# A hybrid attention and expert block: the steps of a block put in another order on TensorE, VectorE and ScalarE

## What is computed

```python
x = x + window_attention(group_norm(x))      # windows of 8x8 tokens, 12 heads of 8, softmax
t = to_tokens(x)
t = t + linear_attention(layer_norm(t))      # feature map exp(t) or t+1 on k and v; k^T v per image and head
t = t + mixture_of_experts(layer_norm(t))    # 4 experts, top 2, gelu, hidden width 384
```

```python
attn = softmax(einsum('wntd,wnsd->wnts', q, k) * SCALE)
out = einsum('wnts,wnsd->wntd', attn, v) @ w_proj + b_proj
```

## Time and profile before

| | us |
|---|---|
| runs shown | 718.61, 720.95, 728.96 |
| median | 720.95 |
| the profiled execution, whole | 715.83 |
| its span, first to last instruction | 714.1 |
| PE / VectorE / ScalarE / GpSimd busy in it | 627.9 / 530.8 / 472.0 / 99.8 |
| granted TensorE clock, mean of the span | 0.962 |

### The profile page before, as it was taken

The page is one execution under the profiler, slowest core; times in us unless marked ns, Lnnn a source line. Parts: engine busy times, 40 slices in busy tenths (PEclk is TensorE's granted clock), DMA queues, the critical chain, the costliest instruction groups (busy, mean ns, idle before and its releaser), DMA issues.

```text
span 714.1 us, 19890 instructions
## 1 busy us (share of the span) xinstructions
PE 627.9 (88%) x6885; PEld 476.8 (67%) x6885; DVE 530.8 (74%) x1364; ACT 472.0 (66%) x843; POOL 99.8 (14%) x146
## 2 busy tenths in 40 slices
PE   1557789899999999999998779999999999999996
PEld 1235576677667776767776667677777777777774
DVE  6334577677777887778976676788878778888875
ACT  1235657557766777766776546877777777777773
POOL 5000122210222211222101311000000000001000
PEclk9999869979999999999999859999999999999999
DMA  2447644463555545456542003122222221222210
GB/s 43 93 100 154 117 85 89 75 114 82 100 97 91 109 101 101 95 84 116 100 90 34 1 5 89 45 56 62 58 58 58 55 55 55 55 55 55 62 48 22
DMA packets 53452, 52.99 MB, mean 74 GB/s; under 512 B 38761, under 2 KB 48811, under 8 KB 51884
## 3 DMA queue, kind: packets, MB, share of 16 engines
q1 hardware_dynamic: 53420, 52.57, 35.2%
HBM read 39.24 MB, written 12.71 MB: 73 GB/s over the span
## 4 chain that ended last, share of the span: by engine, by line
PE 64%; DVE 15%; DMA 8%; SPq 5%; issue 4%; POOL 2%; ACT 1%; DVEq 0%; ACTq 0%; POOLq 0%
PE ps L787 12%; PE ps L789 12%; PE ps L788 12%; SPq L393 5%; DMA k_split<-parts_dram 5%; DVE neg_max L1183 4%; PE ps L659 3%; PE ps L680 3%; PE ps L742 2%; PE ps L752 2%; PE ps L712 2%; DMA parts_dram<-parts_room 2%; PE ps L781 2%; PE ps L632 2%; PE ps L726 2%
## 5 line engine op out<-in xcount | busy, mean ns | idle before, releaser
L1469 DVE TENSOR_TENSOR hidden_part<-hidden,hidden_part 128x512 fp32r<-128x512 f32 x192 | 139.6, 746 | 53.3 <-ACT hidden_part L1104 41.0
L1103 ACT ACTIVATE hidden<-ps 128x512 f32<-128x512 f32 x192 | 115.1, 600 | 62.7 <-PE ps L789 62.7
L1104 ACT ACTIVATE hidden_part<-ps 128x512 fp32r<-128x512 f32 x192 | 113.9, 593 | 0.0
L987 ACT ACTIVATE probs<-ps 128x768 f32<-128x768 f32 x64 | 51.9, 811 | 52.0 <-PE ps L680 52.0
L787 PE MATMUL ps<-in_part,up_part 97*128 97x512 f32 x192 | 78.9, 411 | 0.0
L787 PE MATMUL ps<-hidden_part,down_part 128*96 128x512 f32 x192 | 76.7, 399 | 1.7 <-DVE hidden_part L1469 1.6
L788 PE MATMUL ps<-in_part,up_part 97*128 97x512 f32 x192 | 76.8, 400 | 0.0
L1183 DVE TENSOR_REDUCE neg_max<-ps 128x12 f32<-128x768 f32 x64 | 60.8, 950 | 21.1 <-PE ps L659 20.9
L789 PE MATMUL ps<-in_part,up_part 97*128 97x512 f32 x192 | 76.2, 397 | 0.0
L789 PE MATMUL ps<-hidden_part,down_part 128*96 128x512 f32 x192 | 75.9, 395 | 0.0
L788 PE MATMUL ps<-hidden_part,down_part 128*96 128x512 f32 x192 | 75.4, 393 | 0.0
(11 more groups left out here) (161 smaller groups left out, 1223.0 us busy)
## 6 DMA issues: line engine op xcount, KB each, us to landing
mix_rows<-mix_dram SPq DMA_DIRECT2D x16, 768.0 KB, 5.0
parts_dram<-parts_room SPq DMA_DIRECT2D x32, 288.0 KB, 2.8
q_packed<-parts_dram SPq DMA_DIRECT2D x96, 96.0 KB
k_split<-parts_dram SPq DMA_DIRECT2D x192, 48.0 KB
x_in<-in_x SPq DMA_DIRECT2D x64, 48.0 KB, 4.3
x_res<-in_x SPq DMA_DIRECT2D x64, 48.0 KB, 4.2
out<-out_sb SPq DMA_DIRECT2D x64, 48.0 KB, 1.9
t_all<-in_L_ffn_w SPq DMA_DIRECT2D x2, 576.0 KB
```

Of the source, the lines that this page charges most:

```text
L987: act.activation(probs[p % 2][:, :, :].rearrange("p (b h) t -> p b (h t)", b=2), pT_ps, ACT.Exp, scale=SCALE).then_inc(probs_ready, 1)
L1103: act.activation(hidden[n % 4][:, :], up_ps[n % 4], ACT.Gelu).then_inc(hidden_ready, 1)
L1104: act.activation(hidden_parts[n % 4][0][:, :], up_ps[n % 4], ACT.Gelu).then_inc(hidden_part1, 1)
L1469: dve.tensor_tensor(hidden_parts[n % 4][1][:, :], hidden[n % 4][:, :], hidden_parts[n % 4][0][:, :].bitcast(F32), ALU.subtract).then_inc(h ...
```

## The change

Only the order of the calls in the three `iteration` functions is changed. No instruction is added or taken away, and no semaphore, buffer or wait value changes.

- PE: `oT1` 0 before `max_transpose` 0; `attn_sum` and `shifted_scores` 0 before `scores_of` 2; `max_transpose` 1 before `scores_of` 3; `shifted_scores` 1 before `y1`; `max_transpose` 2 before `gvar`; `shifted_scores` 2 before `pv` 0; `max_transpose` 3 and `pv` 2 before `q_proj`; `shifted_scores` 3 before `h1_transpose`; `k_proj` before `gate`.
- ScalarE: `exp_kv` 1 before `copy_v` 0, `second_part` 1 behind `copy_v` 0; `exp_probs` 0 before `copy_xT`; `pack_max` 3 before `first_part` 0.
- VectorE: `third_part` 0 first, `third_part` 1 from behind `max_parts` 0 to behind `normalise` 0; `features` 0 before `max_parts` 0, `features` 1 before `maxima` 1; `mask_attn` before `maxima` 2; `max_parts` 3 from behind `norm2` to ahead of `residual1`.

```diff
--- before.py
+++ after.py
@@ -812,36 +812,36 @@
                 when(project, v_proj, *j, 0)
                 when(tail_a, pv, *a, 3)
                 when(attend, scores_of, k, u, 1)
+                when(tail_a, oT1, *a, 0)
                 when(attend, max_transpose, k, u, 0)
-                when(tail_a, oT1, *a, 0)
                 when(project, v_proj, *j, 1)
+                when(tail_b, attn_sum, *b)
+                when(attend, shifted_scores, k, u, 0)
                 when(attend, scores_of, k, u, 2)
-                when(tail_b, attn_sum, *b)
                 when(norm, x_transpose, *n)
                 when(tail_a, oT1, *a, 1)
-                when(attend, shifted_scores, k, u, 0)
                 when(tail_b, attn_times_proj, *b)
+                when(attend, max_transpose, k, u, 1)
                 when(attend, scores_of, k, u, 3)
-                when(attend, max_transpose, k, u, 1)
                 when(tail_b, fold, *b)
                 when(tail_a, oT2, *a)
                 when(norm, gmean, *n)
+                when(attend, shifted_scores, k, u, 1)
                 when(tail_b, y1, *b)
+                when(attend, max_transpose, k, u, 2)
                 when(norm, gvar, *n)
-                when(attend, shifted_scores, k, u, 1)
                 when(tail_a, y0, *a)
-                when(attend, max_transpose, k, u, 2)
+                when(attend, shifted_scores, k, u, 2)
                 when(attend, pv, k, u, 0)
-                when(attend, shifted_scores, k, u, 2)
                 when(attend, pv, k, u, 1)
+                when(attend, max_transpose, k, u, 3)
+                when(attend, pv, k, u, 2)
                 when(norm, q_proj, *n)
                 when(tail_b, h2_transpose, *b)
-                when(attend, max_transpose, k, u, 3)
-                when(attend, pv, k, u, 2)
+                when(attend, shifted_scores, k, u, 3)
                 when(tail_a, h1_transpose, *a)
+                when(norm, k_proj, *n)
                 when(tail_b, gate, *b)
-                when(norm, k_proj, *n)
-                when(attend, shifted_scores, k, u, 3)
                 when(tail_a, kv, *a, 0)
 
 
@@ -1047,19 +1047,19 @@
                         step(*args)
 
                 when(tail_a, exp_probs, *a, 3)
+                when(project, second_part, *j, 0)
                 when(tail_b, exp_kv, *b, 0)
-                when(project, second_part, *j, 0)
+                when(tail_b, exp_kv, *b, 1)
+                when(project, copy_v, *j, 0)
                 when(project, second_part, *j, 1)
-                when(project, copy_v, *j, 0)
-                when(tail_b, exp_kv, *b, 1)
                 when(attend, pack_max, k, u, 0)
                 when(project, copy_v, *j, 1)
                 when(tail_a, copy_o, *a, 1)
                 when(drained, exp_gate, 0)
                 when(drained, input_part, 0, 0)
                 when(drained, input_part, 1, 1)
+                when(attend, exp_probs, k, u, 0)
                 when(norm, copy_xT, *n)
-                when(attend, exp_probs, k, u, 0)
                 when(tail_b, copy_aproj, *b)
                 when(attend, pack_max, k, u, 1)
                 when(tail_a, copy_oT, *a)
@@ -1067,9 +1067,9 @@
                 when(attend, pack_max, k, u, 2)
                 when(attend, exp_probs, k, u, 2)
                 when(attend, copy_o, k, u, 0)
+                when(attend, pack_max, k, u, 3)
                 when(norm, first_part, *n, 0)
                 when(tail_b, copy_h2T, *b)
-                when(attend, pack_max, k, u, 3)
                 when(tail_a, copy_h1T, *a)
                 when(norm, first_part, *n, 1)
 
@@ -1341,18 +1341,18 @@
                     if there:
                         step(*args)
 
+                when(project, third_part, *j, 0)
                 when(attend, maxima, k, u, 0)
+                when(tail_b, features, *b, 0)
                 when(attend, max_parts, k, u, 0)
-                when(project, third_part, *j, 0)
-                when(project, third_part, *j, 1)
-                when(tail_b, features, *b, 0)
+                when(tail_b, features, *b, 1)
                 when(attend, maxima, k, u, 1)
-                when(tail_b, features, *b, 1)
                 when(attend, max_parts, k, u, 1)
                 when(drained, gate_shift, 0)
                 when(tail_a, normalise, *a, 0)
+                when(project, third_part, *j, 1)
+                when(tail_b, mask_attn, *b)
                 when(attend, maxima, k, u, 2)
-                when(tail_b, mask_attn, *b)
                 when(drained, gate_softmax, 0)
                 when(tail_a, normalise, *a, 1)
                 when(norm, gn_stats_of, *n)
@@ -1363,10 +1363,10 @@
                 when(norm, gn_spread_of, *n)
                 when(tail_b, residual2, *b)
                 when(norm, gn_var_of, *n)
+                when(attend, max_parts, k, u, 3)
                 when(tail_a, residual1, *a)
                 when(norm, gn_apply, *n)
                 when(tail_b, norm2, *b)
-                when(attend, max_parts, k, u, 3)
                 when(tail_a, norm1, *a)
                 when(drained, gate_rank, 0)
                 when(norm, rest_of, *n, 0)
```

## The result

| | before | after |
|---|---|---|
| median of the runs, us | 722.15 (4 runs) | 754.78 (4 runs) |
| ratio to before | | 1.055, 95% interval 1.045 to 1.065 |
| profiled execution / its span, us | 715.83 / 714.1 | 751.98 / 750.3 |
| mean granted clock | 0.962 | 0.914 |
| steady blocks 5 to 13, us | 21.73 to 21.92, mean 21.75 | 23.3 to 26.2, two kinds in turn |

The account below looks back on a forecast made before the run. k's trip through DRAM was to set steady blocks at 5.65 + 2.6 + 14.5 + 0.05 = 22.8 us, with clock falls on top; +18 on the profiled 715.83 gave 733.8, put on the 720.95 median 739 us, range 722 to 746.

Parts of the forecast that it names:

- the load phase: SP's q and k loads, from the first load's issue to the last landing: 14.5 us in each block.
- the weight of the clock's falls: Granted clock falling after long PE waits: most falls counted, +18 us taken between +9 (none) and +22 (after every one).
- the first blocks: Blocks 0 to 2: block 1 starts 0.9 us later, block 2 gets it back from its slack, total 0.
- End of the third part: VectorE's third part of k ends 5.65 us into a fast block, against 3.14 before, and 7.55 into a slow one.
- Store and issue: From the end of k's third part to the first load on SP's queue: 2.6 us instead of 2.97.
- the fast blocks: Steady blocks at full clock, set by DMA: 22.8 us each, with PE waiting 1.9 us for k.
- slack: Kernel before, steady block: packed k is there 1.1 us before PE asks for it at the next first scores.
- The slow blocks: Steady blocks hit by a clock fall: 24.7 us by DMA, a wait of 0.3 behind, in turn with fast ones.
- The price of a fall on PE: What block 4 took above its neighbours: 3.5 us, so a slow block on PE would be 24.4 us.
- the case with all falls: Blocks 5 to 13 as five fast and four slow ones: 212.8 us instead of 195.8, +17.0.
- Rival B: Attention blocks: DMA sets them but the clock mostly stays, as by the skill's table; +9 us, 730 us; chance 0.25.
- Rival C: Steady blocks: k lands early enough, so PE alone sets them at 20.9 us; −11 us, 710 us; chance 0.12.

Follow-up runs that it names:

- experiment 2: Kernel before with one move alone, the third part of k behind `normalise` 0 on VectorE: 758.29 us, ratio 1.049.
- experiment 1: Changed kernel with the third part of k back behind `max_parts` 0 and its second part back behind that of q: 717.08 us, ratio 0.992.
- experiment 4: Changed kernel with both second parts first on ScalarE behind `exp_probs` and both third parts first on VectorE: 715.63 us, ratio 0.987.
- experiment 5: Changed kernel with the x loads cut from 128 rows to 16 behind the first blocks: 746.87 us, one execution.
- experiment 6: Changed kernel with each k load halved in bytes, the number of loads unchanged: 695.08 us, one execution.
- experiment 10: Changed kernel with both second parts first on ScalarE and both third parts first on VectorE, measured again: 710.74 us, ratio 0.988.
- experiment 3: Changed kernel with four extra matmuls on TensorE ahead of each block's first scores, inside the wait: 741.86 us, ratio 1.025.
- experiment 7: Kernel before with both third parts ahead of `maxima` 0 on VectorE, ScalarE's order unchanged: 752.02 us, ratio 1.056.

## Why the prediction was right and wrong

**What failed.** The sum gave +18.0 for the profiled execution and it was +36.2 (751.98 against 715.83; the medians differ by 32.6). Of the 18.2 between them about 7.9 is the load phase, put at 14.5 us and measured at 15.3; 4.4 is the weight of the clock's falls; 3.2 is the first blocks, put at nothing; 1.6 is the end of k's third part in slow blocks; 1.2 is the store of block 14 and the end.

**Direction and mechanism: right.** The wait stands where it was put, on k's loads before the first scores; blocks alternate between two kinds; experiment 2 shows that this one move is enough, experiments 1 and 4 that with it taken back the other moves cost nothing.

**The terms of the floor.** End of the third part: 5.65 given, 5.67 measured. Store and issue: 2.6 given, 2.6 measured. The load phase was given as 14.5 and measured as 15.33 in the mean of the fast blocks. This is the first mis-sized term. It came from blocks 0 and 14, the only ones of the kernel before that showed it. A steady block has more x loads in flight than block 14, and experiment 5 shows these to be worth 0.9. But single blocks scatter by as much: block 0 of the kernel before had the x loads too and took 14.5; in the changed kernel blocks 0 and 3 took 13.7 and 13.95, and block 14, with the same loads in flight as block 14 before, 15.10. So why steady blocks lie at 15.3 is shown only in part. The fast blocks took 23.59 in the mean, not 22.8: five of them +4.0. By the same term, the kernel before would have had about 0.3 us of slack and not 1.1; its own trace can't show it.

**The slow blocks**, 24.7 given, 25.88 in the mean of four: 0.8 by the load phase, 0.36 by the third part, which ends 7.9 in, not 7.55. Four of them: +4.7. The price of a fall on PE, 3.5, was said to be what block 4 took above its neighbours; it is so against block 5 only, and 1.9 against block 3 (23.41). It didn't enter the slow block's 24.7, which comes from the transfer. Together the nine steady blocks lost 25.7 (221.47 against 195.78) where the case with all falls had +17.0.

**How often the clock falls.** The mechanism was right, the weight not: I took +18 between +9 (none) and +22 (behind each long wait). It fell behind each wait of 1.1 us and more from block 4 on: before blocks 4, 6, 8, 10, 12, 14 and 15. Rival B, by which the clock would mostly stay, didn't come: it fell behind all of these waits of 1.14 to 3.46 us, with PE at work on both sides, and in experiment 1 behind one of 0.43. The table of the Trainium skill (TensorE: Matmul & The Clock Gate, "What's actually happening"), from which that rival was taken, doesn't foretell these falls, and the measurement decides. The same page's section "HAM oscillation", where the clock is low again behind each wait on DMA, fits the long waits here but not the short ones: those of 0.29 to 0.67 before blocks 7, 9, 11 and 13 brought no fall.

**The first blocks.** Block 3 started 3.4 us later, where I had 0. Block 2 should have lost its delay in its slack; it lasted 29.58 instead of 27.51, with scores 1 waiting 5.0 for `maxima` 0. VectorE's timeline in the changed kernel shows what `maxima` 0 waited for:

```profile
93.23 4.34 DVE L1175 TENSOR_TENSOR parts_room<-rest_room,parts_room 96x512 bf16<-96x512 f32 x1 [2.95 <-ACT parts_room L964]
97.49 0.94 DVE L1183 TENSOR_REDUCE neg_max<-ps 128x12 f32<-128x768 f32 x1
```

The third part of q, which the change put ahead of `maxima` 0, waited 2.95 for ScalarE and then took 4.34 us instead of 0.69. Block 2 is the first of the loop, and there one short step of VectorE was slow before too (3.22 us for a `max_parts` that takes 0.17 elsewhere), but it stood behind `maxima` 0. So `maxima` 0 started 7.05 us into the block instead of 0.75, and the third part of k ended 11.85 in instead of 6.41, more than the slack. Why a step is slow there, no run shows. This move can't be the only cause either: experiment 2, without it, began block 3 3.1 us late too, behind a wait of 3.17 on k before block 2. Blocks 3 and 4 gave back 1.4 where 1.2 was given, by luck: block 3 gave back 1.2 for 0.6, as its k came after a load phase of only 13.95, and block 4 0.25 for 0.6.

**The end.** Block 14: +5.3 for +4.0; 0.6 by the load phase, 0.5 by the store, which took 3.06 to the first load, 0.2 by the third part. Block 15 and what follows: +3.3 for +2.6. Sum: 3.4 − 1.4 + 25.7 + 5.3 + 3.3 = 36.3, the difference of the spans (36.2). Of it 22 was in the prediction as its upper case, 9 is the load phase and the slow blocks' third part in blocks 5 to 13.

**Rival C** (PE alone, blocks of 20.9) was near the right price of the other moves: 20.5 in experiment 6, 20.7 in experiments 4 and 10. It failed by the load phase, as written. The new waits of 0.62 before `max_transpose` 3 and 0.26 before `pv` 2 are there, 0.88 in sum, where one of 0.59 had been given.

## What to carry to other kernels

Before a step is moved later, ask what transfer it starts and when its data is wanted a whole iteration on: the wait shows up far from the move, and a trace in which nobody waits doesn't tell how little slack there is. Take the transfer's length from a place with the same neighbours on the queues, and leave it a margin: here the highest seen before was 14.54 us, and the blocks after gave 13.7 to 15.8. A wait that opens on TensorE is to be priced with the clock's fall behind it, here 9 us beside 17 of waiting; and a gain on the bound engine, here 1.0 us a block, is only real once the path that was just hidden beneath it is shortened too.

## What the hardware showed unasked

The clock's fall doesn't go by the length of one gap alone: it fell behind 0.43 us (experiment 1, block 10) and 1.10 (experiment 3, block 6), and not behind 2.04 (experiment 2, block 13), 1.47 (experiment 1, block 12), 0.85 in the kernel before or seven waits of 0.6 to 1.15 in experiment 3. Behind waits of 2.2 us and more before steady blocks it always fell, and in experiment 7 it fell in each of the nine steady blocks behind a wait of only 1.42 or 1.43 on VectorE, in the middle of PE's work. In experiment 5, loads issued later seem to have slowed those issued earlier on the same queue, by 0.9 us of 15.3. And a quarter of the packed bytes taken off, 288 of 1152 KB, all from the k loads, shortened the load phase by 3 us or more in steady blocks and by 4.1 or more in block 14 (experiment 6), while the number of loads stayed.
